# Where the running maxima stand in an attention kernel's steps, and the order of its tail

## The reference

```python
# layer 0: softmax attention, 16 heads of 16 channels
xn = layer_norm(x, norm_w, norm_b)
q, k, v = xn @ q_w + q_b, xn @ k_w + k_b, (xn @ v_w + v_b) * mask
att = softmax(einsum('bnhl,bmhl->bnmh', q, k) + (1 - mask) * -1e6, axis=2)
y = einsum('bnmh,bmhl->bnhl', att, v)
scale, shift = split(silu(cond) @ emb_w + emb_b, 2)
x = x + silu(layer_norm(y) * (1 + scale) + shift) @ out_w + out_b
# layer 1: linear attention, 8 heads of 32 channels
q = softmax(xn @ Wq + bq, over a head's channels)
k = softmax(xn @ Wk + bk + mask term, over tokens)
y = q @ (k.T @ v), per head; then the same modulation, silu and projection
```

## Time and profile before

| | |
|---|---|
| Median of 3 runs | 665.94 us (665.83 to 666.95) |
| Profiled execution | 663.26 us, its span 661.5 us |
| PE, PEld, DVE, ACT, POOL busy | 568.3, 273.5, 446.4, 334.5, 66.7 us |
| Share of the span | 86%, 41%, 67%, 51%, 10% |
| Mean granted clock of TensorE | 0.933 |
| The ring's scores (line 841) | the first at 84.8, the last at 584.5 us |
| The tail | from there to 661.5 |

### The profile page before, as it was taken

The page is one execution under the profiler, slowest core; times in us unless marked ns, Lnnn a source line. Parts: engine busy times, 40 slices in busy tenths (PEclk is TensorE's granted clock), DMA queues, the critical chain, the costliest instruction groups (busy, mean ns, idle before and its releaser), DMA issues.

```text
span 661.5 us, 7870 instructions
## 1 busy us (share of the span) xinstructions
PE 568.3 (86%) x2938; PEld 273.5 (41%) x2938; DVE 446.4 (67%) x899; ACT 334.5 (51%) x399; POOL 66.7 (10%) x86
## 2 busy tenths in 40 slices
PE   3528789999999999989999988999889899956966
PEld 2214342333533344444334434554335443514755
DVE  5246854766599988768998866768885785222552
ACT  3111064554566665547667544555575456651430
POOL 2040050000000212000020400000421020002100
PEclk9769779999999998999999988999899899996888
DMA  6378930546200030303030000011001000000001
GB/s 185 77 202 216 270 115 0 131 117 153 63 26 17 11 75 1 75 0 75 2 74 25 2 25 1 1 28 35 20 23 34 33 2 1 1 1 0 0 1 63
DMA packets 18557, 36.14 MB, mean 55 GB/s; under 512 B 3956, under 2 KB 10476, under 8 KB 17496
## 3 DMA queue, kind: packets, MB, share of 16 engines
q1 hardware_dynamic: 18432, 35.62, 21.3%
q10 hardware_dynamic: 88, 0.02, 0.0%
HBM read 20.50 MB, written 14.70 MB: 53 GB/s over the span
## 4 chain that ended last, share of the span: by engine, by line
PE 60%; DVE 26%; DMA 4%; issue 3%; ACT 3%; SPq 3%; POOL 0%; POOLq 0%; DVEq 0%; ACTq 0%
DVE halfmax L993 16%; PE bank L860 16%; PE bank L749 14%; PE bank L728 8%; PE sT L728 4%; PE bank L801 3%; PE sT L841 3%; PE bank L770 2%; DVE stats L912 2%; PE bank L763 2%; PE bank L758 1%; ACT prob L692 1%; DVE xs L1037 1%; PE bank L822 1%; DMA qs<-stack_rows 1%
## 5 line engine op out<-in xcount | busy, mean ns | idle before, releaser
L993 DVE TENSOR_REDUCE halfmax<-bank 128x1 f32<-128x512 f32 x512 | 319.3, 682 | 72.5 <-PE bank L749 71.0
L692 ACT ACTIVATE prob<-sT 128x1024 f32<-128x1024 f32 x256 | 247.7, 1024 | 155.0 <-PE sT L841 154.3
L749 PE MATMUL bank<-ks,qs 50*128 50x512 f32 x512 | 196.8, 498 | 45.4 <-DVE halfmax L993 23.1
L749 PEld LDWEIGHTS bank<-ks,qs 50*128 50x128 f32 x512 | 79.3, 189 | 179.1 <-DVE halfmax L993 114.1
L860 PE MATMUL bank<-prob,vp 128*17 128x512 f32 x1024 | 139.7, 618 | 0.6 <-ACT prob L692 0.6
L841 PE MATMUL sT<-qs,ks 52*128 52x512 f32 x512 | 97.2, 415 | 5.7 <-DMA qs<-crows 3.7
L554 POOL TENSOR_TENSOR rstd<-var,neghalf 128x4 f32<-128x4 f32 x14 | 14.2, 1013 | 535.5 <-DVE var L922 535.5
L841 PEld LDWEIGHTS sT<-qs,ks 52*128 52x128 f32 x512 | 53.1, 190 | 19.7 <-ACT prob L692 8.4
L728 PE MATMUL bank<-w,hT 128*128 128x256 f32 x144 | 38.8, 406 | 0.0
L728 PEld LDWEIGHTS bank<-w,hT 128*128 128x128 f32 x144 | 27.0, 204 | 13.9 <-DVE halfmax L993 8.3
L860 PEld LDWEIGHTS bank<-prob,vp 128*17 128x17 f32 x1024 | 17.0, 95 | 34.1 <-issue 24.8
(11 more groups left out here) (133 smaller groups left out, 468.5 us busy)
## 6 DMA issues: line engine op xcount, KB each, us to landing
stack_rows<-late SPq DMA_DIRECT2D x16, 512.0 KB, 6.7
ks<-stack_rows SPq DMA_DIRECT2D x16, 384.0 KB
qs<-stack_rows SPq DMA_DIRECT2D x32, 192.0 KB, 3.4
stack_rows<-late SPq DMA_DIRECT2D x16, 256.0 KB, 5.7
out_x<-xs SPq DMA_DIRECT2D x4, 512.0 KB, 2.9
xs<-in_x SPq DMA_DIRECT2D x4, 256.0 KB, 3.9
xs<-in_x SPq DMA_DIRECT2D x2, 512.0 KB, 5.6
late<-in_L_cond_emb_w SPq DMA_DIRECT2D x1, 1024.0 KB, 8.4
```

The lines of the kernel that those rows point to most:

```text
L692: act.activation(prob[:, c % 2, 2 * u:2 * u + 2, :].rearrange("p j n -> p (j n)"), sT[u][:, :], ACT.Exp).then_inc(exp_done, 1)
L749: last = pe.matmul(o, qs[rows, s % SLOTS, c, t * P:(t + 1) * P], ks[rows, hg, c, half * HALF:(half + 1) * HALF], start=True, stop=True)
L993: dve.tensor_reduce(halfmax[:, s % 2, r, half:half + 1], o, axis=AX.X, op=ALU.max, negate=True).then_inc(u.done, 1)
```

## The change

Maxima are no longer spread as two and two over each step. `places(k)` gives four places in a step: before the scores, after them, after the values, and last, two of them in the banks of `sT[0]` once the exponential of u = 0 has read them ("lent" banks, with semaphores of their own; the next step's scores of u = 0 wait for VectorE to have read them). The counts are 1, 2, 0, 2 where a larger unit stands in the step, and 2, 1, 0, 0 or 2, 0, 1, 0 elsewhere; a loop then raises or cuts them so that every group's maxima are complete in time and none starts too early. VectorE takes the maxima of the first two places before `dve_mid`. The planner's numbers are spaced by 64 instead of 16.

In the tail, `keep_busy` issues products of `ident` with a weight into `B8[7]`, which nothing reads: five after the ring, four after the last "out0", three after the last "y1". The tail's units use the seven other banks. The last transposes and output units go by halves in turn, and VectorE takes the third "y1" between the statistics and z of the first half.

```diff
...
         ring_ready, ring_act, ring_dve = sem("ring_ready"), sem("ring_act"), sem("ring_dve")
+        lent_ready, lent_done = sem("lent_ready"), sem("lent_done")
         end_ready, end_act, end_dve = sem("end_ready"), sem("end_act"), sem("end_dve")
...
         stream = [("max", s, m) for s in range(SUBS) for m in range(MAXES)]
-
-        def maxima(k, p):
-            at = AHEAD + 4 * k + 2 * p
-            return stream[at:at + 2]
...
                 dve_at[begins["T", kind, b, h, KC - 1] + 1].append(("silu", kind, b, h))
+        def places(k):
+            kinds = [key[0] for key in pe_at[k]]
+            if any(kind not in SMALL and kind not in ("y", "neg") for kind in kinds):
+                return [1, 2, 0, 2]
+            return [2, 0, 1, 0] if len(kinds) > 1 else [2, 1, 0, 0]
+        LEAD, MOST = 2, 5
+        runs, taken_to = [], AHEAD
+        for k in range(STEPS):
+            s, c = divmod(k, NT)
+            count = places(k)
+            most = min(len(stream), MAXES * (s + 2 + int(c >= 3))) - taken_to
+            least = max(min(len(stream), MAXES * ((k + f + 1 + LEAD) // NT + 1)) - taken_to - MOST * f for f in range(min(2 * NT, STEPS - k)))
+            total = max(min(sum(count), most), min(least, MOST))
+            for place_of in (3, 2, 1, 0):
+                while sum(count) > total and count[place_of] > 0:
+                    count[place_of] -= 1
+            for place_of, limit in ((0, 3), (2, 3), (1, 3)):
+                while sum(count) < total and count[place_of] < limit:
+                    count[place_of] += 1
+            ends = [taken_to + sum(count[:i + 1]) for i in range(4)]
+            runs.append([stream[first:end] for first, end in zip([taken_to] + ends[:3], ends)])
+            taken_to = ends[3]
+        assert taken_to == len(stream)
+        def maxima(k, p):
+            return runs[k][p]
         def dve_step(k):
...
                 return dve_mid[k] + dve_at[k]
-            return maxima(k, 0) + dve_mid[k] + maxima(k, 1) + dve_at[k]
+            return maxima(k, 0) + maxima(k, 1) + dve_mid[k] + maxima(k, 2) + maxima(k, 3) + dve_at[k]
         LNS = [("in0", b, h) for b in range(B) for h in range(NH)]
...
         for h in range(NH):
-            end_order += [("T", "mid1", b, h, kc) for kc in range(KC)]
-        end_order += [("out1", b, s) for s in range(4)]
+            end_order += [("T", "mid1", b, h, kc) for kc in range(KC)] + [("out1", b, 2 * h + i) for i in range(2)]
         act_end = [("T", "mid0", b, 1, kc) for kc in range(KC)] + [("T", "in1", b, 1, kc) for kc in range(KC)]
...
         dve_end += [("qsum", b, 1), ("recips", b)] + [("att", b, kc) for kc in range(KC)]
-        dve_end += [("y1", b, 0), ("y1", b, 1)] + dve_layer("mid1", 0) + [("y1", b, 2), ("y1", b, 3)] + dve_layer("mid1", 1)
+        norm = dve_layer("mid1", 0)
+        dve_end += [("y1", b, 0), ("y1", b, 1)] + norm[:-1] + [("y1", b, 2)] + norm[-1:] + [("y1", b, 3)] + dve_layer("mid1", 1)
         dve_end += [("out1", b, s) for s in range(4)]
...
         for k in range(STEPS):
-            in_ring += maxima(k, 0) + maxima(k, 1) + pe_at[k]
+            in_ring += maxima(k, 0) + maxima(k, 1) + maxima(k, 2) + pe_at[k]
         in_ring.append(("y", SUBS - 1))
...
             for j, key in enumerate(now + also):
-                taken[key] = 16 * k + j
+                taken[key] = 64 * k + j
             dve_order += now
...
         dve_order.append(("y", SUBS - 1))
-        taken["y", SUBS - 1] = 16 * (STEPS + 2)
+        taken["y", SUBS - 1] = 64 * (STEPS + 2)
         place(pro_order, B8[0:4], pro_ready, [key for key in pro_order if key[0] in ON_ACT], [key for key in pro_order if key[0] == "qk"], pro_act, pro_dve)
         place(in_ring, B8[5:8], ring_ready, act_order, dve_order, ring_act, ring_dve, taken)
-        place(end_order, B8[0:8], end_ready, [key for key in act_end if key in end_order], [key for key in dve_end if key in end_order], end_act, end_dve)
+        lent, lent_after = [], []
+        for k in range(STEPS):
+            lent += maxima(k, 3)
+            lent_after.append(len(lent))
+            for j, key in enumerate(maxima(k, 3)):
+                unit[key] = Unit(B8[j], lent_ready, lent.index(key) + 1, lent_done, lent.index(key) + 1, None)
+        place(end_order, B8[0:7], end_ready, [key for key in act_end if key in end_order], [key for key in dve_end if key in end_order], end_act, end_dve)
         def cell(m):
...
                     pe.wait_ge(exp_done, 2 * (k - 1) + u + 1)
+                    if u == 0 and lent_after[k - 1] > 0:
+                        pe.wait_ge(lent_done, lent_after[k - 1])
                 for two in range(2):
...
                     values(k - 1)
+                for key in maxima(k, 2):
+                    fill(key)
+                if maxima(k, 3):
+                    pe.wait_ge(exp_done, 2 * k + 1)
+                for key in maxima(k, 3):
+                    fill(key)
                 for key in pe_at[k]:
...
             values(STEPS - 1)
+            def keep_busy(n):
+                for i in range(n):
+                    pe.matmul(B8[7], ident[:, :], wv0[:, :, :].rearrange("p k d -> p (k d)"), start=True, stop=True)
+            busy = {("y", SUBS - 1): 5, ("out0", b, 3): 4, ("y1", b, 3): 3}
             fill(("y", SUBS - 1))
...
             pe.wait_ge(ring_act, len(act_order))
+            keep_busy(busy["y", SUBS - 1])
             for key in end_order:
                 fill(key)
+                keep_busy(busy.get(key, 0))
         @block.vector
...
```

## The result

The changed kernel takes 632.0 us (630.67 to 640.52, 4 runs) against 665.88 for the one before on the same chip: ratio 0.9487 [0.9458, 0.9517], 33.9 us less. Medians here are over all executions, ratios and their intervals over the fast ones alone; of the four above, 640.52 is a slow one. The forecast was 630.6. The profiled execution has a span of 628.8 us against 661.5 and a mean granted clock of 0.948 against 0.933.

A forecast was written before the change was run, and what follows sets the result against it. The prediction took TensorE's program order plus one wait for a bank as the bound. From 663.26 us it took 26.8 (ring) and 8.6 (tail), giving 627.9, and added 2.7 for the median: 630.6; 620 to 647 at 8 in 10.

The forecast's parts named there:

- Light steps with three: 59 ring steps without a larger unit lose their fourth maximum: 0.47 us less each, -24.3 us after deductions, bounds -15 and -30.
- Rival 2: Light ring steps stop at 2.5 us, held by ScalarE or the query maxima's DMA: 16 us more, 646 us; chance 0.09.
- Light steps with five: 17 light ring steps forced to catch up take a fifth maximum, VectorE setting the pace: +6.5 us, between +3 and +10.
- Heavy steps: 42 ring steps with a larger unit take five maxima in new places: -9.0 us together, bounds -14 and +12.
- Wide maximum: Two keys steps in the ring where VectorE also reduces a 1024 wide maximum: from 16.0 to 10.9 us, -5.1.
- Tail: After the ring, unread products hold the clock and the order goes by halves: -8.6 us, bounds -3 and -10.
- Stage one: First of the tail's three stages, transposes and two output units: 9.7 us becomes about 6.3, -3.4.
- Stage two: Second of the tail's stages: two keys units go from 6.42 to 3.85 us, transposes -0.4, together -3.0.
- Rival 3: Heavy ring steps pay for the fifth maximum, each 0.3 us slower: 21 us more, 652 us; chance 0.09.
- Rival 4: TensorE is full, its 86% busy being work: the ring keeps its length, only the tail gains, 657 us; chance 0.04.
- Rival 5: Scores wait for lent banks in every heavy ring step, 1.2 us each: +50 us instead of -9, 690 us; chance 0.03.
- Rival 1: The tail's clock isn't held, so the tail gains only 3 us: 636 us; chance 0.16.

The follow-up runs named there:

- e1: The changed kernel with the tail put back to its old order, eight banks and no unread products; 642.35 us, 0.9695 of the kernel before.
- e5: The changed kernel without the unread products, keeping the tail's new order and seven banks; 637.43 us, 0.9573 of the kernel before.
- e12: The changed kernel, unchanged, measured again on another chip; 632.24 us, 0.9524 of the kernel before.
- e6: The changed kernel with four maxima in every step: light steps in the old places, heavy ones 1, 1, 0, 2 with lent banks; 627.71 us, 0.9443 of the kernel before.
- e9: The changed kernel with the tail's last part in the old order, keeping the unread products and seven banks; 640.14 us, 0.9589 of the kernel before.

## Why the prediction was right, and where not

*Light steps with three: -24.5 for -24.3.* The size is right, with two errors in it that cancel: the forecast's single maximum was too dear, and steps bound by the exponential were left out. That they cancel so closely is luck; over the 50 steps at full clock the gain is 0.49 a step, which would be 28.8 for all. A clean step takes 2.11, not 2.20: I priced the single maximum ahead of the values at 0.42, from a row where it had waited for its bank; one that didn't wait costs 0.33 (182.42 to 182.75). Others take 2.3 to 2.5, since the second scores wait for the exponential, as the 0.06 of slack that I named let one fear. Rival 2 is there, in some steps. Its other part, the query maxima's DMA, is there too: five waits, 4.2 us of weight load and 2.4 us of matmuls in all, where 0.6 had been taken off. The way itself kept its length, 2.58 from issue (207.54) to scores (210.12) where it was 2.6.

*Light steps with five: +7.6 for +6.5.* The sign held, at a lower price: 0.30 a step at full clock, 5.0 for all. The 7.6 holds a fall of the clock at 253.1, which made two of them 4.9 and 5.5 long.

*Heavy steps: -7.8 for -9.0.* qk 5.04 for 5.03. The v step came out at 5.00, as forecast, against 4.85:

```profile
169.22 0.49 PE L784 MATMUL bank<-ks,qs 50*128 50x512 f32 x1
...
174.22 0.50 PE L784 MATMUL bank<-ks,qs 50*128 50x512 f32 x1
```

Wide maximum 10.4 for 10.9 (16.0 before). The other forty, which I had counted in groups of like steps, gave 2.2 for the 3.9 forecast, and 1.7 of that stands in two output steps where the clock of the kernel before was at half. Where it was full in both, a heavy step moved by -0.02: the fifth maximum ate what the new places gave. Only three of the eight qk steps gained just the 0.17 that I had read from one, and the eight together 0.7 and not 1.4; among the rest are steps where the next scores wait for the lent banks.

*Tail: -9.4 for -8.6.* Stage one gained 3.7 (forecast 3.4) and the last part 3.9 (3.3). Stage two gained 1.7 (3.0), because the clock fell at 584.2, after a wait of 1.32, eight transposes and a wait of 1.10: the fall for which 1.1 had been taken off, in the place that I left open. Part of the early stages' 5.4 isn't the edit's, as e1 shows: 2.2 of it came with no edit there. Of the bounds, "-3 (only the order helps)" was wrong as a mechanism: e5 shows that the order alone gives nothing at half clock. The Trainium skill's rule in "TensorE: Matmul & The Clock Gate", section "A second HAM failure mode: psum-queue depth-cycling", that short pauses between groups let the clock swing, held in one place of the tail and not in the others. Pauses of 1.0 to 1.2 around the transposes at 571, 613 and 618 left the clock at 1.00, and those of 1.3 and 1.1 around the transposes at 582 didn't. In e12, the same program, the same pauses of 1.3 and 1.1 left it at 1.00, and those of 1.0 and 1.2 at 616 and 618 didn't. So the length of a pause doesn't tell, in these traces, which one costs the clock.

*Before the ring: +1.6, forecast 0.* TensorE's mean granted clock from 30 to 60 us was 0.56, and 0.77 before. Nothing that stands there was edited, and the first scores start anywhere from 83.9 to 87.4 in the kernels above.

*The reason, though.* The forecast said: moving the fourth maximum from light steps to heavy ones gains 0.47 there and costs next to nothing here. The numbers were nearly right, yet the reading of them was not, since I compared heavy steps of five in new places with heavy steps of four in old ones. Two edits were in that term. The new places alone take 27.2 us off (e6), and the fifth maximum gives 19.4 of them back. The rule that I weighed, the Trainium skill's "Perfetto Trace Analysis", section "Identifying the Most-Contended Engine", to work on the engine with the highest occupancy first, named the right engine, and the same section's doubt about matmul busy time was in place: TensorE's work even grew by the unread products, 32.7 us went, 23.7 of them out of its idle time, and its share rose by three points.

Rival 3 has its mechanism, since a heavy step does pay 0.47 for the fifth maximum, but not its price: the new places pay for it, and heavy steps got no longer. Rival 4 is out, as the ring got shorter. Rival 5's wait is there in six steps; at 386.76 it was half a us and not 1.2. Rival 1 held for one stretch of 3.4 us.

## What to carry to other kernels

When an edit both moves instructions and changes how many stand in a step, price each by itself: here the moving alone held the ring's whole gain (ring steps 446.9 in e6, 448.4 after, 473.1 before). A producer that must wait for a slow reader belongs behind the instructions that others wait for, and ahead of a long unit that covers the reading; the rows of e6's qk step show this, though the runs don't part it from the two smaller edits that came with it. Unread products to hold the clock pay only where no long wait is left between them and the work (4.63 us in e9 undid them), so they and the order have to be planned together. To compare two profiles, take the same steps, and only those at full clock in both.

## What the runs showed that I had not expected

The same kernel's profiled span was 628.8 in one execution and 633.5 in another (e12): TensorE ran at half clock for 10.2 us at 253.0 and 10.2 us at 369.1 in the second. Over the steps at full clock in both, the two agree to 0.01 us a step. Differences of a few us between profiles are worth nothing unless the same steps show them. And a maximum in front of 128-row work cost 0.33 where it started on time (182.42), but 0.42 or 0.43 where it had waited for its bank (320.71, 132.31); whether the wait is the cause was not tried.
